# Output projection of units 2 to 7 of a Mamba and butterfly-FFN block from plain fp32 to three products of rounded parts

## What is computed

```
x = x + ssm(layernorm(x))
x = x + ffn(layernorm(x))

ssm:  x_inner, z = split(x @ in_proj_w.T)            # 512 channels each
      x_conv = silu(causal depthwise conv, 4 taps)
      delta, B, C = x_conv @ x_proj_w.T              # 1 + 16 + 16
      h = h * exp(delta * A) + x_t * delta * B       # 16 states a channel, over the tokens
      y = (h . C + x_conv * D) * silu(z)
      return y @ out_proj_w.T                        # 512 -> 256
ffn:  h = gelu(butterfly(x @ W_exp + b_exp) + up_bias)          # 1024
      return butterfly(h) @ W_con + b_con + down_bias
```

## Time and profile before

| | |
|---|---|
| median of 3 runs | 543.49 us (543.46 to 544.0) |
| the profiled execution | 543.8 us |
| its span, first to last instruction | 542.1 us |
| PE busy | 516.0 us (95%), mean granted clock 0.981 |
| DVE busy | 416.8 us (77%) |
| ACT busy | 307.0 us (57%) |
| POOL busy | 93.3 us (17%) |
| DMA | 21.75 MB, mean 40 GB/s |
| chain that ended last | PE 58%, DVE 20%, ACT 9%, issue 9% |

### The profile page before, as it was taken

The page is one execution under the profiler, slowest core; times in us unless marked ns, Lnnn a source line. Parts: engine busy times, 40 slices in busy tenths (PEclk is TensorE's granted clock), DMA queues, the critical chain, the costliest instruction groups (busy, mean ns, idle before and its releaser), DMA issues.

```text
span 542.1 us, 8227 instructions
## 1 busy us (share of the span) xinstructions
PE 516.0 (95%) x3012; PEld 422.5 (78%) x3012; DVE 416.8 (77%) x892; ACT 307.0 (57%) x537; POOL 93.3 (17%) x88
## 2 busy tenths in 40 slices
PE   4989999998999999999999999999999999889997
PEld 3756776776887788878888788888888789578886
DVE  4778999888984999489975999489956986576542
ACT  2777883794249622875269722964278514951242
POOL 4040200220211202140211211030213021122020
PEclk9995988999999999999999999999999999999999
DMA  9652511200112001210112002110021001200011
GB/s 223 134 28 3 83 39 41 66 16 2 39 40 76 6 2 50 69 41 1 40 40 81 0 2 79 54 28 2 0 79 42 1 1 39 81 0 1 1 40 39
DMA packets 42635, 21.75 MB, mean 40 GB/s; under 512 B 26435, under 2 KB 41027, under 8 KB 42596
## 3 DMA queue, kind: packets, MB, share of 16 engines
q1 hardware_dynamic: 39956, 17.57, 13.9%
q10 hardware_dynamic: 2640, 3.67, 2.4%
HBM read 16.78 MB, written 4.46 MB: 39 GB/s over the span
## 4 chain that ended last, share of the span: by engine, by line
PE 58%; DVE 20%; ACT 9%; issue 9%; POOL 2%; DMA 1%; DVEq 0%; ACTq 0%; POOLq 0%
PE wide L715 11%; PE acc L877 11%; PE wide L866 9%; PE wide L855 9%; DVE xc L1516 5%; PE wide L829 4%; DVE state L1621 3%; PE small L705 3%; PE wide L840 2%; ACT xc L1186 2%; DVE diag_sum L1639 2%; DVE diag L1635 2%; DVE hid_low L1533 1%; PE wide L725 1%; PE small L735 1%
## 5 line engine op out<-in xcount | busy, mean ns | idle before, releaser
L1146 ACT ACTIVATE hid_f<-wide,bias_up 128x512 f32<-128x512 f32 x64 | 43.9, 686 | 160.5 <-PE wide L866 157.5
L1516 DVE SCALAR_TENSOR_TENSOR xc<-xi,taps,xc 128x512 f32<-128x512 f32 x96 | 96.2, 1007 | 4.5 <-ACT xc L1177 2.3
L877 PE MATMUL acc<-w_down_high,hid_high 128*128 128x256 f32 x256 | 73.7, 288 | 3.5 <-DVE hid_low L1533 3.4
L877 PE MATMUL acc<-w_down_high,hid_low 128*128 128x256 f32 x256 | 72.0, 281 | 0.0
L877 PE MATMUL acc<-w_down_low,hid_high 128*128 128x256 f32 x256 | 72.0, 281 | 0.0
L1533 DVE TENSOR_TENSOR hid_low<-hid_f,hid_high 128x512 fp32r<-128x512 f32 x64 | 47.4, 743 | 15.5 <-ACT hid_high L1259 15.2
L855 PE MATMUL wide<-w_out,xc 128*128 128x256 f32 x256 | 58.4, 388 | 0.7 <-DVE xc L1660 0.5
L715 PE MATMUL wide<-xnT_ln1T_high,w_in_high 128*128 128x512 f32 x128 | 56.7, 443 | 0.0
L877 PEld LDWEIGHTS acc<-w_down_high,hid_high 128*128 128x128 f32 x256 | 48.3, 188 | 10.2 <-issue 6.6
L866 PE MATMUL wide<-xnT_ln2T_high,w_up_high 128*128 128x512 f32 x128 | 54.2, 424 | 1.7 <-DVE xnT_ln2T_low L1527 1.7
L855 PEld LDWEIGHTS wide<-w_out,xc 128*128 128x128 f32 x256 | 49.2, 194 | 7.8 <-issue 1.1
(11 more groups left out here) (193 smaller groups left out, 1035.3 us busy)
## 6 DMA issues: line engine op xcount, KB each, us to landing
x_res<-in_L_attn_x_dram SPq DMA_DIRECT2D x9, 512.0 KB, 3.5
c_near<-c_of_tokens SPq DMA_DIRECT2D x8, 512.0 KB
x_ln<-in_L_attn_x_dram SPq DMA_DIRECT2D x7, 512.0 KB, 3.6
out_dram<-x1b_xn SPq DMA_DIRECT2D x7, 512.0 KB, 2.9
xc<-in_L_attn_in_proj_w_dram ACTq DMA_DIRECT2D x2, 512.0 KB, 7.1
xc<-in_L_ffn_W_exp_dram ACTq DMA_DIRECT2D x1, 1024.0 KB, 11.1
x1b_xn<-in_L_ffn_W_con_dram ACTq DMA_DIRECT2D x1, 1024.0 KB, 15.0
raw_out<-n_L_attn_out_proj_w_dram ACTq DMA_DIRECT2D x1, 512.0 KB, 7.7
```

The costliest lines, as they stand in the source:

```text
L877: last = pe.matmul(acc[:, c, :], hid[h][:, j % HRING, c * P:(c + 1) * P], w_down[w][:, j, 0:DM], start=j == 0 and c % 2 == 0 and n == 0, s ...
L1146: ins = act.activation(out_ap, in_ap, how.pop("func"), **how)
L1516: ins = dve.scalar_tensor_tensor(xc[u % BATCH][:, e, :], xi[:, e, tap:tap + TILE], taps[:, e, tap:tap + 1], xc[u % BATCH][:, e, :], ALU.mu ...
```

## The change

The output projection of units 2 to 7 is computed as `up` and `down` are: data and weights are split into a rounded high part and a rounded low part, and the projection is three products of the rounded type where it was one plain fp32 product. It keeps its place in PE's program.

- ACT makes the high part of `xc` in pairs of blocks (128 x 1024): `high_of_gated(u, 0)` between `gelu(p, 3)` and `gelu(p, 4)`, `high_of_gated(u, 1)` behind `high_parts(r, "ln1T")`, ahead of `gelu(p, 5)`. Each waits for `gated` of its pair.
- DVE makes the low part: `low_of_gated(u, 0)` behind `low_hidden(p, 2)`, ahead of `first_normalise(r)`; `low_of_gated(u, 1)` behind `low_hidden(p, 3)`, ahead of `convolve(v, 2)`. Each waits for the high part of its pair. In phase 7 they stand behind `gates_of_halves(u, 0)` and `(u, 1)`.
- PE waits for both low parts (`y_low_ready`) where it waited for `gated`.
- The weights' parts are made once, in phase 1: the high part by ACT behind `gelu(p, 4)`, the low part by DVE behind `low_hidden(p, 7)`, ahead of `final(p)`.
- No memory is added: `y_low` lies over `xc`, `y_high` over `z`, the weights' parts over `con_mixed`, which is dead after phase 1.

```diff
--- before.py
+++ after.py
@@ -181,8 +181,12 @@
         xnT = {name: [sb(f"xnT_{name}_{part}", [P, MB, TILE], F32R) for part in PARTS] for name in ("ln1T", "ln2T")}
         xi = sb("xi", [P, CB, HALO + TILE])
         halo = [sb(f"halo{b}", [P, CB, HALO]) for b in range(BATCH)]
-        xc = [sb(f"xc{b}", [P, CB, TILE]) for b in range(BATCH)]
-        z = [sb(f"z{b}", [P, CB, TILE]) for b in range(BATCH)]
+        with ExitStack() as under_gated:
+            xc, z = ([under_gated.enter_context(nc.sbuf_tensor(f"{name}{b}", [P, CB, TILE], F32)) for b in range(BATCH)]
+                     for name in ("xc", "z"))
+            con_mixed = under_gated.enter_context(nc.sbuf_tensor("con_mixed", [P, HB, DM], F32))
+        y_low, y_high = ([sb(f"y_{part}{b}", [P, CB, TILE], F32R) for b in range(BATCH)] for part in ("low", "high"))
+        w_out_r = [sb(f"w_out_{part}", [P, CB, DM], F32R) for part in PARTS]
         x_tok = sb("x_tok", [P, GR, DI])
         state = [sb(f"state{b}", [P, DI]) for b in range(BATCH)]
         state_end = [sb(f"state_end{b}", [NS, DI]) for b in range(BATCH)]
@@ -308,6 +312,10 @@
         states_ready = Signal(sem("states_ready"), 1)
         skipped = Signal(sem("skipped"), CB)
         gated = Signal(sem("gated"), CB)
+        y_high_ready = Signal(sem("y_high_ready"), CB // 2)
+        y_low_ready = Signal(sem("y_low_ready"), CB // 2)
+        w_out_high = sem("w_out_high")
+        w_out_low = sem("w_out_low")
         x1b_ready = Signal(sem("x1b_ready"), 1)
         hid_high = Signal(sem("hid_high"), HB)
         hid_ready = Signal(sem("hid_ready"), HB)
@@ -342,7 +350,6 @@
         pathT = x_res[:, :, :].rearrange(flat).rearrange("p (g j) -> p g j", j=P)
         partial = x1[:, :, :].rearrange(flat)
         raw_con = x1b_xn2[:, :, :, :].rearrange("p a b d -> p (a b) d")
-        con_mixed = sb("con_mixed", [P, HB, DM])
         high_w = [sb(f"high_w{i}", [P, HIGH, HB // 2, 4]) for i in range(2)]
         bias_raw = c_hat[:, :].rearrange("p (n d) -> p n d", d=DM)
         up_bias_sb = sb("up_bias_sb", [P, HB])
@@ -847,6 +854,17 @@
             def out_projection(u, h):
                 bank = tile_of("out", h, u)
                 free(pe, u, "out", h)
+                if u >= HALVES_FROM:
+                    if h == 0:
+                        pe.wait_ge(w_out_low, 1)
+                        wait(pe, y_low_ready, u - HALVES_FROM, CB // 2)
+                    y = (y_high[u % BATCH], y_low[u % BATCH])
+                    for q in range(2):
+                        for n, (g, w, x) in enumerate((g, w, x) for g in range(CB) for w, x in PASSES):
+                            last = pe.matmul(bank[:, q * DM:(q + 1) * DM], y[x][:, g, (2 * h + q) * P:(2 * h + q + 1) * P],
+                                             w_out_r[w][:, g, :], start=n == 0, stop=n == CB * len(PASSES) - 1)
+                    mark_written(last, "out", h, u)
+                    return
                 if h == 0:
                     wait(pe, gated, u, CB)
                 for q in range(2):
@@ -1198,6 +1216,19 @@
                     written(act, u, "y", CB - 1, ago=1)
                 take(u, "xtok", c, x_tok[:, c, :], tile_of("xtok", c, u)[:, :])
 
+            def high_of_gated(u, pair):
+
+                blocks = slice(2 * pair, 2 * pair + 2)
+                wait(act, gated, u, 2 * pair + 2)
+                act.activation(y_high[u % BATCH][:, blocks, :], xc[u % BATCH][:, blocks, :], ACT.Copy)\
+                    .then_inc(y_high_ready.handle, 1)
+
+            def high_of_w_out():
+
+                for q in range(4):
+                    wait_taken(act, ("w_down", q, 0))
+                act.activation(w_out_r[0][:, :, :], w_out[:, :, :], ACT.Copy).then_inc(w_out_high, 1)
+
             def load_exp_table(place=0):
 
                 act.activation(tables[:, place:place + 1], ones[:, 0:1], ACT.Exp)
@@ -1347,9 +1378,14 @@
                     beside("gelu 1")
                 gelu(p, 2)
                 gelu(p, 3)
+                if u >= HALVES_FROM:
+                    high_of_gated(u, 0)
                 gelu(p, 4)
+                beside("gelu 4")
                 if r < UNITS:
                     high_parts(r, "ln1T")
+                if u >= HALVES_FROM:
+                    high_of_gated(u, 1)
                 gelu(p, 5)
                 gelu(p, 6)
                 gelu(p, 7)
@@ -1366,6 +1402,8 @@
                     prepare(16)
                 elif place == "gelu 1":
                     prepare(17)
+                elif place == "gelu 4":
+                    high_of_w_out()
 
             prepare(0)
             high_parts(0, "ln1T")
@@ -1681,6 +1719,19 @@
                     read(dve, u, "y", 2 * pair + h)
                 for g in (2 * pair, 2 * pair + 1):
                     dve.tensor_tensor(own[:, g, :], own[:, g, :], z[u % BATCH][:, g, :], ALU.mult).then_inc(gated.handle, 1)
+
+            def low_of_gated(u, pair):
+
+                blocks = slice(2 * pair, 2 * pair + 2)
+                wait(dve, y_high_ready, u - HALVES_FROM, pair + 1)
+                dve.tensor_tensor(y_low[u % BATCH][:, blocks, :], xc[u % BATCH][:, blocks, :],
+                                  y_high[u % BATCH][:, blocks, :].bitcast(F32), ALU.subtract).then_inc(y_low_ready.handle, 1)
+
+            def low_of_w_out():
+
+                dve.wait_ge(w_out_high, 1)
+                dve.tensor_tensor(w_out_r[1][:, :, :], w_out[:, :, :], w_out_r[0][:, :, :].bitcast(F32), ALU.subtract)\
+                    .then_inc(w_out_low, 1)
 
             def first_residual(u, h):
                 if h == 0:
@@ -1794,10 +1845,12 @@
                     first_stats(r)
                 gates_of_halves(u, 0)
                 low_hidden(p, 2)
+                low_of_gated(u, 0)
                 if r < UNITS:
                     first_normalise(r)
                 gates_of_halves(u, 1)
                 low_hidden(p, 3)
+                low_of_gated(u, 1)
                 convolve(v, 2)
 
             def to_last_outputs(u):
@@ -1851,6 +1906,8 @@
                 second_normalise(u)
                 low_hidden(p, 6)
                 low_hidden(p, 7)
+                if u == 1:
+                    low_of_w_out()
                 if v == UNITS:
                     low_parts(u, "ln2T")
                 final(p)
```

## The result

| | before | after |
|---|---|---|
| median of the runs compared | 543.48 us (543.34 to 544.0) | 575.9 us (575.27 to 575.97) |
| ratio | | 1.0588, interval 1.0575 to 1.06 |
| span of the profiled execution | 542.1 us | 574.1 us |
| mean granted clock | 0.981 | 0.958 |

The changed kernel is slower, by 32.4 us. The forecast was 571, with a range of 558 to 579.

The account below looks back on a forecast made before the run. The prediction took PE to bound the kernel, busy 59.02 of 59.60 us a phase. To 543.8 us it added 21.9 for the projection's lateness less PE's saving, and 5.5 for the clock: 571 us, range 558 to 579.

Parts of the forecast that it names:

- The saving on PE: Output projection of units 2 to 7: rounded products save PE 1.14 us a unit, 6.8 in all.
- The count of passes: Projection on PE: four passes for true FP32 against three rounded would save a quarter, 1.68 us a unit; not adopted.
- the row of `down`: PE's products of the same shape in `down`, 0.1186 us each, giving 5.69 us for the projection's 48.
- PE sets the time: Steady phase: PE is busy 59.02 of 59.60 us, so any wait of PE is paid in full.
- PE only gains: Rival: projection's parts are ready in time, so 543.8 - 6.8 = 537 us; chance 0.03.
- The split's chain: From gates through copy and subtraction to PE: 5.2 us late in units 2 to 5, 3.8 in 6, 4.1 in 7.
- The rival that it would not hold up the low part: POOL's bias addition does not delay DVE's pair 1 subtraction; units 1.4 to 1.6 us better, 559.4 in all; chance 0.12.
- Behind the projection: After the projection, DVE reaches the first residual before PE needs it for `up` 6; nothing added, nothing won back.
- The weights' parts: Phase 1: ACT's copy and DVE's subtraction fall into waits and cost nothing; uncovered, 1.07 + 1.22 us once.
- The clock: PE's granted clock falls around the long gaps before the projection: 1.1 us in five units, 5.5; bounds 0 and 17.
- the clock stays low for longer: Rival: two low-clock stretches a unit, 12 us or more in place of 5.5, 578 to 583 us; chance 0.12.
- The sum: Whole kernel: 543.8 + 21.9 net lateness + 5.5 clock = 571.2 us.

## Why the prediction was right

- **The saving on PE.** Forecast 1.14 us a unit. At the full clock it is 6.72 - 5.84 = 0.88 in the projection and 0.25 behind it, 1.13. The count of passes would have given 1.68; the row of `down` was the better guide. But the step had a gap that the new wait hid: "PE sets the time" was read from its busy share, so that a saving on PE would pass into the time. In the old place all but 0.2 us of it does not, since PE then waits for DVE. In this kernel, with PE late, the saving did pass. That the gap cost nothing was luck. The rival "PE only gains", put at 537, was out of reach in this order for that reason too: with no split at all it is 540.9.
- **The split's chain.** Forecast 5.2, 3.8 and 4.1 us late in units 2 to 5, 6 and 7; measured 5.13 to 5.20 and 3.95; in unit 7 the projection is 4.80 late, 1.21 of it from `down` 4 at the lower clock, so `down` 4 itself starts 3.6 late, 0.5 less than forecast. That is the 2.35 us that POOL's addition took there, where the sum had 2.76. By parts in unit 3: copy 1.06 (1.07), subtraction 1.23 (1.22), the gates of pair 1 later by (270.66 - 264.02) - (262.79 - 257.87) = 1.72 (1.9), the subtraction under POOL 2.77 (2.8), and 0.15 from its end to PE's start, which the sum left out. The 0.18 too much and the 0.15 left out cancel, which is luck: the 5.2 is closer than its parts.
- **POOL.** The rival that it would not hold up the low part fell: 1.23 and 2.77 in the trace, and again when POOL was moved.
- **Behind the projection** nothing was added, as forecast, and nothing won back beyond the 0.25 that the rounded type saves. The weights' parts cost nothing, as forecast: PE's stretch from the projection of unit 1 to the next phase is 18.61 us, 18.62 before.
- **The clock** is the term that was mis-sized. Forecast 5.5 us, 1.1 in five units. Against 5.84 the projections lost 2.36, 1.86, 1.47, 1.50, 2.28 and 0.07, and `down` 4 of unit 7, 2.72 us long where it was 1.51, lost 1.21: 10.75 in all. The experiment with products in the wait took back 8.5 of it by the spans (574.1 - 565.6); it leaves unit 7's wait alone, where `down` 4 lost the same 1.21 and the projection 1.08. The forecast took 1.4 us for one fall from the earlier trace rows and rebated it to 1.1, in five units, for falls that would not come or would end inside the wait. Three things were off. All six came. In three of them the clock stayed low twice as long, as the windows show (units 2, 3 and 6, then 4, 5 and 7; columns as above):

```profile
208.60:215.40 6.80, 5.42 (x25) 5.45 (x26) 6.66 (x9) 0.00 (x0) 0.15 (x1) 0.50 0.00 0
273.50:280.30 6.80, 4.31 (x20) 4.34 (x21) 6.66 (x8) 0.00 (x0) 1.26 (x1) 0.50 0.06 22
468.00:474.80 6.80, 5.16 (x24) 5.19 (x25) 6.43 (x8) 0.00 (x0) 0.42 (x1) 0.50 0.00 0
341.70:345.10 3.40, 3.40 (x18) 3.40 (x18) 3.29 (x6) 0.00 (x0) 0.00 (x0) 0.50 0.00 0
406.60:410.00 3.40, 3.40 (x16) 3.40 (x17) 3.29 (x6) 0.00 (x0) 0.00 (x0) 0.50 0.00 0
529.40:532.80 3.40, 2.97 (x14) 2.97 (x15) 0.97 (x2) 0.00 (x0) 0.00 (x0) 0.51 0.00 0
```

The long ones, each of which began 1.4 to 2.5 us before PE's wait ended, cost 2.36, 1.86 and 2.28 us, the short ones 1.47, 1.50 and 1.28: 1.8 on average. And the price of one was read a little low. The window of the earlier trace rows begins 0.6 us behind the fall; the stretch from 87.40 to 90.80 has a clock of 0.51. Beside it, the same products behind the same wait happened to keep the full clock in the changed kernel's profile (from 87.04 to 94.12, where before they took from 87.35 to 96.11):

```profile
87.04 7.15 PE L873 MATMUL wide<-w_out,xc 128*128 128x256 f32 x32 [0.45 <-DVE xc L1698]
94.12 1.94 PE L732 MATMUL wide<-xc,w_x 128*64 128x512 f32 x8
```

So that one fall cost 8.76 - 7.08 = 1.68 us. The term of 10.75 is between the forecast and the rival "the clock stays low for longer", which had put it at 12 or more for two stretches in every unit; it was true of three units out of six.
- **The sum.** 21.9 forecast without the clock, 32.0 - 10.75 = 21.3 measured. The clock's 5.5 against 10.75, less the 0.6 that the rest was too high, leaves the forecast 4.7 us short by the spans, and 4.9 from the rounded 571 to the median. That is inside its range.

## What to carry to other kernels

A cheaper form of an operation is paid for where its operands are made: count the copy and the subtraction on the path from the last producer to PE, not only PE's products, and if that path is already on the edge, move the operation to where the parts are ready before changing its form. Here the same 48 products a unit cost 32 us in the old place (six units) and gained 5.5 in another (five units). Before counting a saving on an engine that is busy 99% of a phase, ask where its in-order neighbour would stop it if the first were faster; leaving the work out and keeping only the new products answers that in one run.

## What the runs showed that was not expected

- **A wait of PE can cost more than its length, and how much more varies.** Behind the transposes of the norm (units 2 to 5), waits of 4.9 us were followed by the lower clock in 4 of 4 units, of 3.4 us in 2 of 4, and of 2.2 us in 2 of 4, the last two with the same order and length from unit to unit. Transposes ahead of the wait are not needed for it: in unit 6 a wait of 2.58 us behind the full-size products of `down` 2 was followed by a fall too, with POOL behind the low part. Of the waits of 1.74 us behind `down` 3, none was, in 4 of 4. What decides which of two equal waits is followed by a fall was not tried and stays open.
- **Useless products can pay.** 180 products that write a bank about to be overwritten saved 8.2 us, because PE had nothing to do there anyway and the clock stayed up.
